# Attention stage of a fused block on one core: two transposed tiles and the router products stand one projection later, and a weight maximum is taken in eight pieces

## What is computed

```python
h = _layernorm(x) * (1 + ca) + sa
xn = rmsnorm(h, gamma)
q, kv, a = split(xn @ w_qkva.T)          # three projections of 512 each
kv_scan = scan(s[t] = sigmoid(a[t]) * s[t-1] + kv[t])
x = x + ga * (q * kv_scan)
h = _layernorm(x) * (1 + cb) + sb
probs = softmax(h @ Wr); top 2 experts, position in each expert by a running count
hid = relu(buf @ W1[e] + b1[e]);  y = hid @ W2[e] + b2[e]
x = x + gb * (weighted sum of the two y of a token)
```

## Time and profile before

| what | value |
|---|---|
| median of 3 executions | 2143.46 us (2142.52 to 2143.86) |
| the profiled execution | 2144.93 us |
| its span, first to last instruction | 2142.7 us |
| granted PE clock, mean | 0.999 |
| PE busy | 2112.4 us (99%) |
| DVE busy | 1783.5 us (83%) |
| ACT busy | 1061.3 us (50%) |
| POOL busy | 381.4 us (18%) |

### The profile page before, as it was taken

The page is one execution under the profiler, slowest core; times in us unless marked ns, Lnnn a source line. Parts: engine busy times, 40 slices in busy tenths (PEclk is TensorE's granted clock), DMA queues, the critical chain, the costliest instruction groups (busy, mean ns, idle before and its releaser), DMA issues.

```text
span 2142.7 us, 35624 instructions
## 1 busy us (share of the span) xinstructions
PE 2112.4 (99%) x13294; PEld 1256.9 (59%) x13294; DVE 1783.5 (83%) x3029; ACT 1061.3 (50%) x2098; POOL 381.4 (18%) x335
## 2 busy tenths in 40 slices
PE   7999999999999999999999999999999999999998
PEld 2454444545474657656764766576466657656676
DVE  7799989999888887887888779778877987887754
ACT  5465666767372645355253625534461644356250
POOL 1134343443424010100001010101101010100101
PEclk9999999999999999999999999999999999999999
DMA  8899996775675642553264345416434542553212
GB/s 290 247 261 247 243 239 165 188 167 123 157 196 155 195 116 58 146 149 99 34 213 120 79 119 152 123 26 192 104 99 97 175 123 51 165 132 99 37 15 25
DMA packets 353212, 301.05 MB, mean 141 GB/s; under 512 B 242475, under 2 KB 242731, under 8 KB 352528
## 3 DMA queue, kind: packets, MB, share of 16 engines
q1 hardware_dynamic: 331136, 256.63, 43.1%
q0 software_dynamic: 21904, 42.14, 10.2%
HBM read 163.84 MB, written 93.01 MB: 120 GB/s over the span
## 4 chain that ended last, share of the span: by engine, by line
PE 91%; DVE 3%; DMA 1%; issue 1%; SPq 1%; ACT 0%; POOLq 0%; DVEq 0%; another core or an unknown queue 0%; ACTq 0%
PE bank L2161 32%; PE bank L2244 19%; PE bank L2077 18%; PE bank L2254 9%; PE bank L2281 5%; PE bank L2272 4%; PE bank L2149 2%; DMA reg_e<-reg_e 1%; PE bank L2026 1%; SPq L581 1%; DVE reg_e L1365 0%; DVE reg_e L1377 0%; PE bank L2037 0%; PE bank L2039 0%; DVE reg_e L1248 0%
## 5 line engine op out<-in xcount | busy, mean ns | idle before, releaser
L2077 PE MATMUL bank<-reg_c 128*128 128x512 f16 x2296 | 505.4, 379 | 1.7 <-ACT reg_e L961 1.2
L2161 PE MATMUL bank<-reg_e,reg_a 128*128 128x320 f16 x2880 | 447.5, 299 | 0.0
L2244 PE MATMUL bank<-reg_b,reg_c 128*128 128x512 f16 x1872 | 406.5, 379 | 0.0
L2077 PEld LDWEIGHTS bank<-reg_c 128*128 128x128 f16 x2296 | 222.0, 98 | 259.3 <-ACT reg_e L961 1.6
L2161 PEld LDWEIGHTS bank<-reg_e,reg_a 128*128 128x128 f16 x2880 | 280.9, 98 | 112.7
L2244 PEld LDWEIGHTS bank<-reg_b,reg_c 128*128 128x128 f16 x1872 | 182.9, 98 | 218.9 <-DVE reg_e L1611 2.0
L845 POOL DMA_INDIRECT out_dram<-reg_e,midx x79 | 141.3, 1789 | 944.6 <-DVE reg_e L1614 871.7
L2161 PE MATMUL bank<-reg_e,reg_d 128*128 128x320 f16 x1440 | 232.5, 299 | 0.0
L1054 ACT ACTIVATE reg_e<-bank,b1s 128x320 f32<-128x320 f32 x120 | 63.3, 527 | 251.4 <-PE bank L2161 250.4
L2161 PEld LDWEIGHTS bank<-reg_e,reg_d 128*128 128x128 f16 x1440 | 139.7, 98 | 57.6 <-ACT reg_e L1054 4.1
L787 POOL DMA_INDIRECT slot_rows<-reg_e,sli x112 | 130.0, 1161 | 101.7 <-DVE reg_e L1439 61.3
(11 more groups left out here) (267 smaller groups left out, 3399.8 us busy)
## 6 DMA issues: line engine op xcount, KB each, us to landing
reg_d<-in_w SPq DMA_DIRECT2D x232, 512.0 KB, 4.8
slot_rows<-zrow SPq DMA_DIRECT2D x32, 516.0 KB, 4.8
reg_b<-in_x SPq DMA_DIRECT2D x16, 1024.0 KB, 7.6
out_dram<-reg_b SPq DMA_DIRECT2D x16, 1024.0 KB, 6.7
reg_d<-in_w SPq DMA_DIRECT2D x8, 1024.0 KB, 9.7
slot_rows<-zrow SPq DMA_DIRECT2D x32, 129.0 KB, 4.6
reg_d<-in_wmod SPq DMA_DIRECT2D x4, 1024.0 KB, 12.0
reg_e<-mod_rows SPq DMA_DIRECT2D x7, 512.0 KB, 9.5
```

Source lines behind the costliest of these rows:

```text
L2077: ins = mm(dst[:, :], wqs[:, ws, kc, e0:e0 + P], xns[:, j % 2, xs, kc, :], start=kc == 0 and xs == 0 and ws == 0, stop=kc == KC - 1 and ws ...
L2161: ins = mm(dst[:, 0:CAP], w[ws][:, c, p * P:(p + 1) * P], xs_of[:, KC * xs + 2 * i + c, j * CAP:(j + 1) * CAP], start=first and c == 0 and ...
L2244: ins = mm(bank_y[i % 2][:, :], hid[:, hs, hc, t * P:(t + 1) * P], w2s[:, ws, hc, :], start=k == 0 and hs == 0 and ws == 0, stop=k == HC - ...
```

## The change

On PE the transposes of tiles 2 and 3 stand after Q0 instead of after KV0, and the router products after A1 instead of after Q0. On DVE `add_y` of tiles 2 and 3 stands after `mix` 0 instead of before it. The four maxima over 128x2048 in blocks 1 to 4 become eight over 128x1024 in blocks 1 to 8; the scale is made in block 9 instead of 4, `b1_scale` in block 10, and ACT's `w_hi_quarter` 0 to 2 in blocks 10 to 12.

```diff
@@ ACT, step
-                if 6 <= i <= 8:
-                    w_hi_quarter(0, 0, i - 6)
+                if 10 <= i <= 12:
+                    w_hi_quarter(0, 0, i - 10)
@@ DVE, step
                 if has(i, 1):
                     apply1(nq, nj, 1)
-                if has(i, -1):
-                    add_y(n - 1, pj, 2)
-                    add_y(n - 1, pj, 3)
...
                 if has(i, 0):
                     mix(q, j, 0)
+                if has(i, -1):
+                    add_y(n - 1, pj, 2)
+                    add_y(n - 1, pj, 3)
                 if has(i, -2):
                     route_choose(oq, oj)
...
-                if 1 <= i <= 4:
-                    w_max_quarter(0, 0, i - 1)
-                if i == 4:
+                if 1 <= i <= 8:
+                    w_max_half(i - 1)
+                if i == 9:
                     w_scale_head(0, 0)
...
-                if i == 4:
+                if i == 9:
                     pm_reduce()
...
-                if i == 4:
+                if i == 9:
                     pm_copy()
                     w_scale_tail(0, 0, 7)
+                if i == 10:
                     b1_scale(0)
...
+            def w_max_half(k):
+
+                c, half = k // 2, k % 2
+                wait(dve, s_stg[c], 16)
+                ins = v_.tensor_reduce(wmx[:, 8 + k:9 + k], stage[:, c, half * 1024:(half + 1) * 1024], AX, ALU.max,
+                                       apply_absolute_value=True)
+                if half:
+                    ins.then_inc(s_wch, 1)
@@ PE, step
-                    if k < 2 and has(i, -1):
-                        turn_y(q, j, 2 * k, i)
-                        turn_y(q, j, 2 * k + 1, i)
-                    if k == 2 and has(i, -2):
+                    if k in (0, 2) and has(i, -1):
+                        turn_y(q, j, k, i)
+                        turn_y(q, j, k + 1, i)
+                    if k == 3 and has(i, -2):
                         for t in range(TB):
                             logits(n - 2, oq, oj, t)
...
-                    if i == 4 and k == 9:
+                    if i == 9 and k == 9:
                         pe.wait_ge(s_wch, 7)
...
-                    if i == 4 and k == 11:
+                    if i == 9 and k == 11:
                         pe.wait_ge(s_pm, 1)
```

More of the change, by code:

```diff
@@ L260, in build_program @@
         b1s = sb("b1s", [P, B, HC], F32)
-        wmx = sb("wmx", [P, 8], F32)
+        wmx = sb("wmx", [P, 16], F32)
         wm = sb("wm", [P, 2, 11], F32)
@@ L1532, in w_scale_head @@
                     lk(5, v_.tensor_reduce(wmx[:, 6:7], b1r[:, :], AX, ALU.max, apply_absolute_value=True))
-                    lk(6, v_.tensor_scalar(wmx[:, 4:5], wmx[:, 6:7], shmax[:, 0:1], None, ALU.mult))
+                    lk(6, v_.tensor_scalar(wmx[:, 7:8], wmx[:, 6:7], shmax[:, 0:1], None, ALU.mult))
+                    lk(7, v_.tensor_reduce(wmx[:, 5:6], wmx[:, 7:16], AX, ALU.max))
                 else:
                     wait(dve, s_wch, WLINKS * e + 11 * which + 4)
-                lk(7 - 2 * which, v_.tensor_reduce(wmx[:, 5:6], wmx[:, 0:5 - which], AX, ALU.max))
-                return 7 - 2 * which
+                    lk(5, v_.tensor_reduce(wmx[:, 5:6], wmx[:, 0:4], AX, ALU.max))
             def w_scale_tail(e, which, k0):
```

## The result

Beside each other, 18 executions each, the changed kernel took 2148.01 us in the median (2143.96 to 2154.87) and the kernel before 2143.14 (2141.07 to 2146.33): a ratio of **1.0022, 95% interval [1.0016, 1.0028]**, 4.9 us slower. The forecast of 2141.9 has the wrong sign, and the time lies outside its range. The profiled execution of the changed kernel took 2147.22 with a span of 2145.0, 2.3 more than the one before. Two executions of the experiments, one of e6 (3742.9 us at a mean granted clock of 0.556) and one of the kernel before beside e8 to e11 (3726.18 at 0.559), were in a slow state and stand in no ratio.

What follows compares the result with a forecast made beforehand. The prediction took PE to bound the attention (33.76 us a block without waits), DVE close behind. Its terms -5.8 + 3.7 + 0.5 = -1.6 us took 2143.5 to 2141.9 us, range 2138.5 to 2146.5.

Steps and rivals of the forecast that it cites:

- 5.8 us are lost in blocks 1 to 14.: Attention blocks 1 to 14: PE's waits lengthen them from 472.0 to 477.80 us; the change wins these 5.8 back.
- Part 1, tiles 2 and 3: PE's transposes after Q0 get 2.59 us more; the waits for `add_y` in blocks 1 and 5 go, at no cost.
- Part 2, the floor at S + 13.1: DVE's `route_choose` never starts before 13.1 us after S, the start of A0, as its router products come 2.59 later.
- Part 3, 3.7 us of waits: Half maxima in DVE's tail make PE wait at the first transposes after blocks 2 to 9, together 3.7 us.
- the gain of 1.3 is lost and 0.5 more: Block 15: router wait of 1.3 us goes, but later `route_choose` moves the last transposes from S + 39.3 to S + 39.9.
- Behind the transposes nothing changes.: After the last transposes, in the handover and the experts, the time stays as before: no term in the sum.
- The rule weighed: Shared SBUF port of DVE and POOL, applied to `rstd1`'s power of 3.50 us in block 4; no term of the sum.
- 1: Full gain: DVE has more slack, old waits go and no new ones come, -7.9, 2135.6 us; chance 0.14.
- 2: POOL becomes late for `apply1` part 1, each time 2.65 us: once 2144.5 (chance 0.11), more often 2147.2 to 2155 (0.07).
- 3: A DVE hiccup like block 7's 2.41 us at `mix` 3's product falls elsewhere: 2143.5 to 2144.3 us; chance 0.09.
- 4: Router DMAs land later with the later `lo2`, half of the DMA waits stay: +1, 2142.9 us; chance 0.04.

Runs made afterwards that it cites:

- e6: Kernel before with only block 15's order changed (tiles 2 and 3 after Q0, router products after A1): 4.0 us over the kernel before, ratio 1.0016.
- e8: Changed kernel with three small DVE reductions ahead of the first large addition of the handover's second half: 4.3 us over the kernel before, ratio 1.0017.
- e11: Changed kernel with block 15 in the order of before, second run: 3.4 us over the kernel before, ratio 1.0014.
- b2: Kernel before, unchanged, profiled once more, one trace: span 2139.4 us.
- e10: Kernel before with zero fills writing 128 bytes of each row instead of 2064: 1.0 us under the kernel before, ratio 0.9997.
- e12: Kernel before with tiles 2 and 3 one projection later in blocks 1 and 5 only: 0.9 us under the kernel before, ratio 0.9997.
- e14: Kernel before with only the maxima in halves and the later scale, second run: 1.3 us over the kernel before, ratio 1.0003.
- e2: Kernel before with only the maxima in halves and the later scale, first run: 1.5 us over the kernel before, ratio 1.0003.
- a2: Changed kernel, unaltered, run again for a second trace: 5.8 us over the kernel before, ratio 1.0024.
- e15: Changed kernel with block 15 in the order of before and zero fills of 128 bytes a row: 0.0 us over the kernel before, ratio 1.0004.
- e5: Changed kernel with the last transposes one piece of expert work (24 products) later: 7.5 us over the kernel before, ratio 1.0038.
- a3: Changed kernel, unaltered, profiled a third time, one trace: span 2145.7 us.
- e7: Changed kernel with later last transposes and router products after Q0 in blocks 2 to 9 and 15: 4.8 us over the kernel before, ratio 1.0024.

## Why the prediction was wrong, point by point

- **"5.8 us are lost in blocks 1 to 14."** The term that failed first. It came from one execution. Without events these blocks take 476.0 (b2, e6) against 472.0 without waits: 4.0 us, which are block 1 and both places of block 5, all set by DVE. (e10 has 476.0 too, with a router wait of 0.59 in block 3 in place of the one at the turn to block 5.) The 0.6 in block 7 and the 0.9 of DMA waits were that execution's.
- **Part 1, tiles 2 and 3.** Right: no wait for `add_y` in any trace with the new order. "Cost nothing" held for A2's sigmoid, but not for what I left out, SP's queue.
- **Part 2, the floor at S + 13.1.** Right, and it was the reason of the waits that recur. `route_choose` starts 0.18 to 0.19 behind its products, in block 15 at 560.66 (S = 547.52, so S + 13.14), where before it was 561.26. What I didn't cost is that x's transposing DMAs stand behind it: 17.2 instead of 15.5, the loss of the margin in block 4.
- **Part 3, 3.7 us of waits.** Right in place and size: 0.33, none, 0.17, 0.50, 0.33, 0.38 and 0.17 in brackets; blocks 1 to 14 take 475.9, which is 3.9 over 472.0. (Block 4's is missing because a DMA wait of 0.32 just ahead gave DVE the time.) Forecast was 0.46, 0.46, 0.28, 0.70, 0.57, 0.56, 0.27, 0.41 in lengths. So 4.0 won and 3.9 paid: **without events blocks 1 to 14 are a draw, not a gain of 2.1**.
- **Block 15, "the gain of 1.3 is lost and 0.5 more".** Forecast at S + 39.9, measured 587.41 - 547.52 = S + 39.9. The other side of the difference was wrong: S + 39.3 held a DMA wait that b2, e10, e12 and e14 don't have; they have 38.0. The term is +1.9.
- **"Behind the transposes nothing changes."** Wrong twice. I forecast a wait of 2.5 to 3.5 and didn't ask what it does to the clock, which costs 1.6 to 1.7 in three of eight traces; and the handover has two switches, thrown by 0.1 us.
- **The rule weighed.** I spent it on the power of `rstd1`, whose 3.50 didn't recur in block 4. The same rule (the Trainium skill, SBUF — State Buffer, "Who interferes with whom": a DVE instruction with two inputs in SBUF contends with a GpSimd instruction that reads SBUF, under an exclusive lock, and the order of issue decides who is blocked) fits the scatters of the handover in every trace, with a fixed 0.84 to 0.86 behind the addition; only in e10, e11 and b2 are the two starts of one switch too close, at most 0.01 apart, to tell which was first.
- **The rivals.** 1 was excluded by the floor, as said. 2: POOL is late for `apply1` part 1 four times (2.1 in total, in blocks 11 to 14), but under the floor, so it costs nothing. 3: gaps without a releaser are real and move, up to 4.06 in e2, but not between the programs. 4 is the nearest: DMA waits stay, and new ones come. None of them had the order of block 15 and the handover in it. **In short, the step that failed** is the sum -5.8 + 3.7 + 0.5 with "nothing" behind it: without events its terms are -4.0, +3.9 and +1.9, so that +1.8 stands where -1.6 was, and the clock and the handover behind the transposes, with late DMAs in block 4, add the rest of the measured 4.9, by amounts that differ from execution to execution. How much of it recurs stays open.

The sum as the traces give it, mean of three of the changed kernel less mean of two of before: start +0.9, blocks 1 to 14 +1.4, block 15 +1.2, clock +1.1, handover +0.8, together +5.4 of span, beside 4.9 and 5.8 in the medians. Steady in it are block 15's 1.9 (against the traces without the router wait). The others are events (a2's block 4, with its own fall of the clock, makes the 1.4), and with so few traces their rates stay open. That the 0.9 ahead of block 1 has to do with the change is not shown: the traces of all versions have 73.5 to 75.7 there. Open too is what makes the weight load land early, which it did in 6 of the 11 traces whose block 15 has tiles 2 and 3 late, and in 1 of the other 9 (e15), counting e8 by its natural start.

## What to carry to other kernels

Moving a product later on a full PE is paid by whoever reads it: count the reader's start as a floor, and then every queue behind the reader, DMA queues included, with the margin that their slowest execution leaves. Take a loss from two traces of the same program before you build a sum on it: here 1.8 + 1.3 us of the waits to be won were not there in the second one. A stretch in which PE starts a chain of other engines is bound by the moment of the start; cover put ahead of it doesn't give that back (e5).

## What the runs showed of the hardware

- A scatter of POOL (an indirect DMA with its indices in SBUF) that starts while DVE adds two SBUF operands ends 0.84 to 0.86 us behind the addition, in all six traces; one that starts 0.07 us ahead of the addition takes its usual 0.97, and DVE's 1.23 don't change. Where the starts lie 0.01 apart (e10), the scatter takes 0.97 and the addition 1.27.
- The granted clock can fall behind a single short wait of PE, and need not. Between 70 and 720 us it fell ten times in the 20 traces, each time behind one wait: three of the eight of 2.67 ahead of the last transposes (0.59 and 0.55 in two windows of 2 us after it, 0.79, 0.50 and 0.85 in a3; 1.00 throughout in e6), and waits for a DMA or for `mix` 3 of 2.82 (a2), 2.56 (e11), 2.06 (e2), 1.86 and 1.51 (e7), 1.35 (e12) and 1.34 (e8). It stayed at 1.00 behind 17 others of 1.29 to 1.97. A fall costs 1.6 to 1.7 us.
- Four transposing DMAs that take 5.4 us in blocks without fills take 9.1 to 11.7 beside the zero fills, and 5.7 to 6.1 when these write 128 bytes a row.
- Two executions of one program differ by 1.2 to 8 us in blocks 1 to 14: 477.8 and 476.0 before, 475.9 and 481.7 after, 483.4 and 475.4 for e2 and e14.
